# A routed two-layer MoE kernel with linear attention: at most two of GpSimd's scatters under way at once

## The reference

```
x = x + 0.5 * moe(layernorm(x))        # layer 0
x = x + attention(layernorm(x))        # 16 heads of 8, decaying linear attention, gate, output product
x = x + 0.5 * moe(layernorm(x))        # layer 1, same weights

def moe(xf):                           # 4096 tokens, 8 experts, hidden width 512
    expert = argmax(xf @ Wr.T + br)    # each token goes to one expert
    h = relu(W1[expert] @ xf + b1[expert])
    return W2[expert] @ h + b2[expert]
```

## Time and profile before

| | |
|---|---|
| runs (us) | 517.29, 519.77, 520.08; median 519.77 |
| profiled execution | 516.73 us, span 514.9 us from first to last instruction |
| busy share of the span | PE 72%, DVE 63%, POOL 47%, ACT 37% |
| mean granted TensorE clock | 0.84 of full speed |
| HBM traffic | 142 GB/s over the span |

### The profile page before, as it was taken

How to read it: one execution, slowest core, us unless ns; L and a number is a source line. 1 busy time by engine, 2 the same in 40 slices (tenths; PEclk the granted TensorE clock), 3 DMA queues, 4 the chain that set the end, 5 groups by cost and what they waited for, 6 DMA issues and landing times. The chain is left out here.

```text
span 514.9 us, 10079 instructions
## 1 busy us (share of the span) xinstructions
PE 369.8 (72%) x2474; PEld 326.2 (63%) x2474; DVE 326.6 (63%) x972; ACT 190.3 (37%) x570; POOL 243.6 (47%) x246
## 2 busy tenths in 40 slices
PE   4484105999999967967969779666499720699983
PEld 2474105999998745646658667555399620599983
DVE  4745002566657389999999998996666700256641
ACT  1160002555555512343544635402365200255540
POOL 1007771455544457637364582657131277245443
PEclk9655556999999979979899897868699975599998
DMA  8993454788886199000000000003566442277840
GB/s 252 364 390 111 147 175 144 225 246 238 231 279 210 42 296 284 1 1 0 1 1 0 1 1 2 0 32 113 182 194 182 139 150 83 79 206 228 243 127 6
DMA packets 55238, 72.17 MB, mean 140 GB/s; under 512 B 6831, under 2 KB 39884, under 8 KB 54928
## 3 DMA queue, kind: packets, MB, share of 16 engines
q1 hardware_dynamic: 46784, 53.95, 35.2%
q0 software_dynamic: 6016, 13.13, 6.9%
q10 hardware_dynamic: 2384, 4.46, 2.3%
HBM read 45.58 MB, written 27.75 MB: 142 GB/s over the span
## 5 line engine op out<-in xcount | busy, mean ns | idle before, releaser
L953 PE MATMUL bank<-slot_xT,w_ring 128*128 128x128 f32 x736 | 103.4, 283 | 14.2 <-issue 8.2
L953 PEld LDWEIGHTS bank<-slot_xT,w_ring 128*128 128x128 f32 x736 | 93.4, 198 | 16.7 <-issue 12.0
L336 POOL DMA_INDIRECT slots_in<-rows,slot_of x64 | 62.4, 975 | 76.8 <-DVE slot_of L695 58.2
L730 DVE TENSOR_SCALAR hT_b<-bank,b_cur 128x128 f32<-128x128 f32 x184 | 56.0, 347 | 45.2 <-PE bank L953 26.7
L1011 PE MATMUL bank<-outer_all,decay_sb 128*128 128x256 f32 x256 | 75.3, 423 | 8.8 <-DVE outer_all L251 4.5
L251 POOL TENSOR_TENSOR outer_all<-qkv 128x512 f32<-128x512 f32 x60 | 63.9, 1100 | 24.6 <-ACT qkv L476 24.6
L346 POOL DMA_INDIRECT out_x<-ring x46 | 44.7, 972 | 64.6 <-DVE ring L737 42.9
L963 PE MATMUL bank<-w_sb,hT_a 128*128 x368 | 59.5, 285 | 18.7 <-DVE ring L737 17.1
L346 POOL DMA_INDIRECT x<-ring x46 | 44.6, 971 | 55.9 <-issue 31.7
L1011 PEld LDWEIGHTS bank<-outer_all,decay_sb 128*128 128x128 f32 x256 | 51.2, 211 | 28.1 <-issue 10.8
L771 DVE TENSOR_REDUCE o_in<-qS 128x64 f32<-128x512 f32 x64 | 68.0, 1073 | 0.0
(11 more groups left out here) (110 smaller groups left out, 491.8 us busy)
## 6 DMA issues: line engine op xcount, KB each, us to landing
w_ring<-in_w1t SPq DMA_DIRECT2D x92, 256.0 KB
slots_in<-fill SPq DMA_DIRECT2D x4, 3128.0 KB, 18.3
ring<-slots_in SPq DMA_DIRECT2D x92, 136.0 KB
rows<-in_x SPq DMA_DIRECT2D x8, 256.0 KB, 6.6
w_sb<-in_w2t ACTq DMA_DIRECT2D x1, 2048.0 KB, 15.3
rows<-x SPq DMA_DIRECT2D x8, 256.0 KB, 4.3
decay_sb<-in_decay ACTq DMA_DIRECT2D x1, 1024.0 KB, 16.6
slots_in<-rows,slot_of POOLq DMA_INDIRECT x64
```

The source lines that it names most:

```text
L336: pool.indirect_dma_start(slots_in[u], bass.IndirectOffsetOnAxis(ap=slot_of[u][:, t:t + 1], axis=0), row_of(u % GROUPS * GROUP_TILES + t), ...
L730: last = nc.vector.tensor_scalar(hT_b[G % 2][:, f * P:(f + 1) * P], bank_b[:, f * P:(f + 1) * P], b1_cur[G % 2][:, 2 + f:3 + f], 0.0, ALU. ...
L953: last = mm(to[:, f * P:(f + 1) * P], w1_ring[G % W1_BUFS][:, (2 * half + f) * P:(2 * half + f + 1) * P], slot_xT[G % 2][:, :], start=True ...
```

## The change

The sort scatters of units 1 and 3 (`u % GROUPS == 1`) are split over two semaphores, even tiles on `rows_sorted[u]` and odd tiles on `odd_rows_sorted[u]`. Before it issues tile t, GpSimd waits until tile t - 2 has landed. The sorts of units 0 and 2 are as they were. Result scatter G waits for result scatter G - 2 instead of G - 12; the 12 semaphores stay. SyncE's first slot load of units 1 and 3 waits for both semaphores.

```
+IN_FLIGHT = 2
...
+        odd_rows_sorted = {u: sem(f"odd_rows_sorted{u}") for u in range(UNITS) if u % GROUPS == 1}
...
                 if first_of_unit(G):
-                    sp.wait_ge(rows_sorted[u], 16 * GROUP_TILES)
+                    if u % GROUPS == 1:
+                        sp.wait_ge(rows_sorted[u], 16 * GROUP_TILES // 2)
+                        sp.wait_ge(odd_rows_sorted[u], 16 * GROUP_TILES // 2)
+                    else:
+                        sp.wait_ge(rows_sorted[u], 16 * GROUP_TILES)
...
                 for t in range(GROUP_TILES):
+
+                    done = odd_rows_sorted[u] if u % GROUPS == 1 and t % 2 == 1 else rows_sorted[u]
+                    if u % GROUPS == 1:
+                        wait(pool, done, 16 * (t // 2))
                     pool.indirect_dma_start(
                         slots_in[u], bass.IndirectOffsetOnAxis(ap=slot_of[u][:, t:t + 1], axis=0),
-                        row_of(u % GROUPS * GROUP_TILES + t), None).then_inc(rows_sorted[u], 16)
+                        row_of(u % GROUPS * GROUP_TILES + t), None).then_inc(done, 16)
...
                     pool.wait_ge(y_done, G + 1)
-                    if G >= SCATTER_SEMS:
-                        wait_scattered(pool, G - SCATTER_SEMS)
+                    if G >= IN_FLIGHT:
+                        wait_scattered(pool, G - IN_FLIGHT)
```

## The result

The changed kernel takes 528.32 us in the median (four runs, 524.62 to 533.91), the kernel before 519.92 beside it. The ratio is 1.0146, with a 95% interval of 1.0084 to 1.0208. (It leaves out the run of 533.91 us, a slow execution with a granted clock of 0.831, where the other three had 0.847 to 0.858.) The change makes the kernel slower by some 8 us. The forecast was 486 us, and 528.32 lies above its range of 477 to 522. The profiled execution took 527.45 us with a span of 525.6 us, 10.7 us more than before.

A forecast was written before the change was run, and what follows sets the result against it. Scatters needing 1.42 us each but issued each 1.27 us were taken to hold up engine signals; 516.73 - 18.8 - 14.6 = 483.3 us profiled, so 486 us median, range 477 to 522.

The forecast's parts named there:

- What bounds the kernel: Holes beside scatter runs: each scatter needs 1.42 us of something shared, is offered each 1.27 us, and engine signals wait.
- Rival B: Unit 0's uncapped sort leaves 2.5 us backlog until 81; first hole gains only 2 us, second 14.6; 503 us, chance 0.20.
- first hole: Layer 0, sorts of units 0 and 1: first W1 product moves from 83.56 to 64.8, 18.8 us gained.
- the way to 532 us: Skill's rule that DMA never contends with compute engines: scatters would not cause the holes, which would stay.
- Spacing of a capped sort: Sorts of units 1 and 3: landing 2.46 plus 0.80 us for two scatters, 1.63 each, taken as 1.60 instead of 1.265.
- the sum: Whole kernel: 516.73 - 18.8 - 14.6 = 483.3 us for the profiled execution, 486 us as median.
- Second large hole: Layer 1, unit 3's sort: slot 66's W1 product starts at 438.1 instead of 452.70, 14.6 us gained.
- The step that failed: Result scatters capped at two: 1.50 us each in a backlog, and no cost at a steady pass's 1.9 us spacing.
- Rival C: Holes come from unbroken sequence or number of scatters, so release still waits for the run's end; 532 us, chance 0.21.
- The signs that I named: Timeline checks: sort scatters 1.5 to 1.65 us apart, first copy near 63, first result scatter near 84, unit 3's load 26.4 us after.
- Unit 2's hole: ScalarE's wait after unit 2's uncapped sort, predicted to stay at about 8 us.

The follow-up runs named there:

- 128 columns: Kernel before plus a memset pause of 128 columns after every sort and result scatter, sort spacing 1.355 us; 520.09 us, ratio 1.0018.
- the kernels with every sort paused: Kernel before plus a GpSimd memset after every sort and result scatter, tiles of 128, 256, 384, 512 columns: 520.09, 513.21, 515.30, 510.37 us.
- the last experiment: Kernel with 384-column pauses after sort scatters of units 1 and 3 and all result scatters (506.67 us), plus results waiting two back: 524.45 us, ratio 1.0161.

## Why the prediction was wrong

**What bounds the kernel: held.** Rival B's rule, 1.42 us for each scatter and no release before the backlog is gone, dates most of the large holes: 1.40 us with half the rows, a large hole at a spacing of 1.355 and none at 1.46, and release at 74.21 where the rule says 74.2. It is not exact. With 128 columns ScalarE was released at 76.69, when 31 scatters had started, for which the rule asks until 34.62 + 31 x 1.42 = 78.6; and within unit 3's run in the kernel before ScalarE was let through once, at 417.07 after 4.05 us. I had set the rule aside for the first hole because "a small backlog seems to be borne". For the first copy it is not: the changed kernel was released at 70.22, not near 63. By the rule the backlog is gone when the 23rd scatter is served, at 37.15 + 23 x 1.42 = 69.8 us, before the 24th starts at 70.91. B itself gave 81 because it made unit 0's backlog too large. It took 1.265 us for unit 0's spacing; by the earlier trace rows the 16 scatters take 58.67 - 37.50 = 21.17 us, 1.32 each, which leaves 22.72 - 21.17 = 1.55 us and not 2.5. At the 1.62 us that the capped scatters then had, (68.07 - 58.36) / 6, eight of them clear it, by about 71. The holes end early once scatters are spaced, without any other change; so the Trainium skill's SBUF — State Buffer, section "Who interferes with whom", which I had weighed as the way to 532 us, does not cover this case.

**Spacing of a capped sort: 1.60 predicted.** Unit 3 has (437.88 - 414.40) / 15 = 1.565 us, as sized. Unit 1 has 1.62 up to 68.07, but (91.40 - 58.36) / 15 = 2.20 over the whole, since its second part ran beside TensorE's pass: a sort scatter too lands later there.

**First hole: 18.8 us predicted, 12.7 measured.** The first product moved from 83.56 to 70.88, right behind ScalarE's copy. The copy waited for unit 0's backlog. The weights were later than predicted too: the first load went out at 64.34 us, about 1.7 us after the 62.6 that the sum has for it.

**Second large hole: 14.6 us predicted, 14.0 measured.** With the sort's start at 414.40 instead of 408.48, the step's 438.1 becomes 444.0; the product started at 444.58.

**The step that failed is that of the result scatters:** "for result scatters in a backlog it is (2.20 + 0.80) / 2 = 1.50 us" and "at the steady 1.9 us spacing the wait is long met (3.8 us against 2.20 + 0.80) and costs nothing". I took the 2.20 us from the last scatter of layer 0, when no pass ran beside it. Where few loads run it is nearly right: the ten last scatters of the changed kernel are (519.30 - 505.21) / 9 = 1.57 us apart. Inside a pass a scatter lands after 3.8 (97.30 - 92.66 - 0.80) to 4.0 us, so two take 4.6 to 4.8 us. That is 2.3 to 2.4 us each against a slot's 1.9. GpSimd fell behind, and the last scatter starts 5.99 us (layer 0) and 14.2 us (the end) after the last result. The wait also bunched the scatters in pairs 1.28 us apart, nearer than 1.42, and TensorE's pace fell beside them; I had expected the pairs but reckoned with their mean alone. The Trainium skill, DMA: Bandwidth & Descriptors, section "Anatomy of one DMA", gives an estimate of 2.15 us for 64 KB. It agrees with the 2.20 alone, not with 4.0 beside the loads; its formula has no term for them.

**In the sum** the two gains of 26.7 us were there, against 33.4 predicted, but 26.7 + 11.1 = 37.8 us were lost elsewhere in the account above, where I had 0. Of these, 15.3 us are layer 0's pass, which takes 109.5 us from first copy to last result instead of 94.2, and 6.1 us the last stretch. Another 4.9 and 13.1 us are scatters that start later behind the last results of the two layers. That makes 39.4; 1.6 us were regained between the layers. How much each cause has in the slower passes (the pairs, and the sort that ran on beside the first) was not taken apart. Without any pairs the landing wait cost some 18 us in the last experiment. The prediction held 3.8 us against a 3.0 that had been read outside the pass. Rival C's 532 us came near the time by another mechanism, so that was luck: its holes that stay did not happen.

**The signs that I named.** Unit 2's hole stayed, at 8.21 us. SyncE's first slot load of unit 3 came 440.37 - 414.40 = 26.0 us after the sort's first scatter (26.4 predicted), and TensorE waited in front of it. The first result scatter came at 92.66 instead of 84.

**Open.** What the scatters and the engines share is not shown by any view; the runs settle its rate, not its name. That it is signals which are held is my reading of "remote". Why 1.57 us still slows a running pass when 1.42 frees a standing one is not shown either. Of the kernels with every sort paused, only part of the shortfall against the forecasts is accounted for.

## What to carry to other kernels

Read the time that a transfer takes to land from the very stretch in which the wait will stand, beside the loads that run there; a wait for "n back" costs nothing only if n spacings exceed that time and the cost of the released wait. If the aim is to space transfers, space them on the issuing engine (506.67 us), not by waiting for landings (528.32 us), and look at the smallest spacing and not only at the mean. And when long waits have no named releaser, divide them by the count of what runs beside them: a constant quotient, here 1.42 us, is a rate to test.

## What the runs showed of the hardware that I had not expected

- Indirect scatters of GpSimd that start less than about 1.42 us apart hold up ScalarE and VectorE, by up to 34.52 us, with no releaser named. The price was 1.40 to 1.43 us per scatter for 128 x 1088 bytes, 64 x 1088 bytes and runs with 128 x 512 bytes among them, while GpSimd issues one each 1.21 to 1.27 us.
- A result scatter of 64 KB lands 2.20 us after its start when the DMA engines are nearly free, and 3.8 to 4.0 us after it beside loads that keep them busy for 0.7 to 0.8 of the time.
- Beside a running pass scatters 1.57 us apart still slow TensorE (59 matmuls in 10 us), and scatters 1.68 us apart hardly do (88), both at a granted clock of 1.00.
